# Field 5 of a recommendation model looked up instead of gathered, with the small tables as the stationary side

## What is computed

```python
wide = dense @ Wd_wide
for si, wi in zip(S, w):
    wide = wide + wi[si]
wide = wide + wc0[S[3] * VOCABS[4] + S[4]]
wide = wide + wc1[S[5] * VOCABS[6] + S[6]]
deep_in = jnp.concatenate([dense @ Wd_deep] + [Ei[si] for Ei, si in zip(E, S)], axis=1)
h = jax.nn.relu(deep_in @ W1)      # 576 -> 512
h = jax.nn.relu(h @ W2)            # 512 -> 256
deep = h @ W3                      # 256 -> 1
return bias + deep + wide
```

## Time and profile before

| what | us |
|---|---|
| median of 3 runs | 231.23 |
| profiled execution, span from first to last instruction | 134.6 |
| difference, outside the span | 96.6 |
| TensorE matmul busy | 108.5 |
| TensorE weight load busy | 88.8 |
| GpSimd busy | 94.8 |
| VectorE busy | 57.8 |
| ScalarE busy | 41.5 |
| mean granted TensorE clock (1 is full speed) | 0.918 |

### The profile page before, as it was taken

The page is one execution under the profiler, slowest core; times in us unless marked ns, Lnnn a source line. Parts: engine busy times, 40 slices in busy tenths (PEclk is TensorE's granted clock), DMA queues, the critical chain, the costliest instruction groups (busy, mean ns, idle before and its releaser), DMA issues.

```text
span 134.6 us, 2035 instructions
## 1 busy us (share of the span) xinstructions
PE 108.5 (81%) x792; PEld 88.8 (66%) x792; DVE 57.8 (43%) x136; ACT 41.5 (31%) x82; POOL 94.8 (70%) x105
## 2 busy tenths in 40 slices
PE   6978793999999999999999999999999998100000
PEld 2956782677888879888888878888878788100000
DVE  4796389218797646365622254322252234000000
ACT  3894653367631113111313313313311123000000
POOL 3688777777878778778777777777877877877400
PEclk9999999599999999999999999999999999755555
DMA  3699485233422223322334322200000000000000
GB/s 97 167 277 178 78 107 103 20 22 28 36 24 26 29 23 32 28 25 25 32 21 33 28 25 27 32 0 1 5 0 0 1 0 0 1 0 0 1 2 0
DMA packets 5993, 5.17 MB, mean 38 GB/s; under 512 B 2955, under 2 KB 4267, under 8 KB 5984
## 3 DMA queue, kind: packets, MB, share of 16 engines
q0 software_dynamic: 3072, 2.15, 20.1%
q1 hardware_dynamic: 2912, 2.90, 7.7%
HBM read 4.87 MB, written 0.17 MB: 37 GB/s over the span
## 4 chain that ended last, share of the span: by engine, by line
POOL 68%; issue 22%; DMA 3%; POOLq 1%; DVE 1%; DVEq 0%
POOL x L315 47%; POOL cross L322 21%; DMA cross<-in_wc_dram,idx_cross 2%; DMA idx_raw<-in_index_dram 1%; POOLq L99 1%; DVE idx_wrap L448 0%; DVE idx_sum L450 0%; DVE idx_look L454 0%; DVE result L623 0%; DVE idx_gather L454 0%; DVEq L622 0%
## 5 line engine op out<-in xcount | busy, mean ns | idle before, releaser
L315 POOL DMA_INDIRECT x<-in_rows_dram,idx_gather x64 | 63.4, 990 | 21.4 <-issue 19.2
L322 POOL DMA_INDIRECT cross<-in_wc_dram,idx_cross x32 | 30.3, 946 | 9.7 <-issue 9.7
L702 PE MATMUL mm_ps<-xt_hi,w_hi 128*128 128x512 f32 x64 | 28.9, 451 | 0.0
L704 PE MATMUL mm_ps<-xt_hi,w_lo 128*128 128x512 f32 x64 | 25.6, 399 | 0.0
L703 PE MATMUL mm_ps<-xt_lo,w_hi 128*128 128x512 f32 x64 | 25.3, 396 | 0.0
L502 DVE SCALAR_TENSOR_TENSOR h_lo<-mm_ps,h_hi 128x512 fp32r<-128x512 f32 x16 | 11.0, 690 | 25.9 <-ACT h_hi L348 25.9
L348 ACT ACTIVATE h_hi<-mm_ps 128x512 fp32r<-128x512 f32 x16 | 9.6, 600 | 35.0 <-PE mm_ps L704 35.0
L671 PE MATMUL look_ps<-table_parts,onehot 128*128 128x65 bf16 (+1 forms) x292 | 18.2, 216 | 2.4 <-ACT x L358 1.4
L671 PEld LDWEIGHTS look_ps<-table_parts,onehot 128*128 128x128 bf16 x292 | 15.5, 98 | 5.7 <-issue 2.9
L496 DVE TENSOR_TENSOR xt_lo<-tr_ps,xt_hi 128x512 fp32r<-128x512 f32 x16 | 11.0, 685 | 18.1 <-ACT xt_hi L342 18.1
L704 PEld LDWEIGHTS mm_ps<-xt_hi,w_lo 128*128 128x128 f32 x64 | 12.2, 190 | 2.7
(11 more groups left out here) (79 smaller groups left out, 100.7 us busy)
## 6 DMA issues: line engine op xcount, KB each, us to landing
x<-in_rows_dram,idx_gather POOLq DMA_INDIRECT x64, 3.3
w_sb<-in_w_dram SPq DMA_DIRECT2D x1, 1024.0 KB
w_sb<-in_w_dram SPq DMA_DIRECT2D x1, 512.0 KB
cross<-in_wc_dram,idx_cross POOLq DMA_INDIRECT x32, 2.4
dense_stack<-dense_dram SPq DMA_DIRECT2D x3, 156.0 KB
table<-in_small_dram SPq DMA_DIRECT2D x1, 195.0 KB, 2.5
table<-in_small_dram SPq DMA_DIRECT2D x1, 162.5 KB, 2.5
dense_dram<-dense_parts SPq DMA_DIRECT2D x1, 156.0 KB
```

The costliest lines, as they stand in the source:

```text
L315: nc.gpsimd.indirect_dma_start(out=x[:, t, g * ROW:(g + 1) * ROW], out_offset=None, in_=big[g], in_offset=bass.IndirectOffsetOnAxis(ap=idx ...
L322: nc.gpsimd.indirect_dma_start(out=cross[:, c, t:t + 1], out_offset=None, in_=wc[c], in_offset=bass.IndirectOffsetOnAxis(ap=idx_cross[:, c ...
L702: nc.tensor.matmul(dst, w_hi, a_hi, start=start, stop=False)
L704: return nc.tensor.matmul(dst, w_lo, a_hi, start=False, stop=stop)
```

## The change

- Field 5 (8 chunks of 128 rows) joins the looked-up fields; the gathers of rows are 48, in the order fields 0 and 1 of a block, then field 2 of it. The cross gathers stay.
- `look_up` is turned round. For a chunk, `table_hl` (64 columns of high parts and 64 of what is left, both fp32r) is stationary and the one-hots of 512 samples move: one fp32r matmul a chunk and block, 76 in all. The bank then holds the embeddings already turned, the high part in partitions 0 to 63 and the low one in 64 to 127, and ScalarE copies both (`looked`) into `xt_hi` and `xt_lo`. `x`, the summing by VectorE and the turns of these fields are gone; turns are two a block.
- The fields' weights are looked up apart (`look_up_wide`): 128 one-hots are stationary, the upper bf16 half of each fp32r element being read by a step of two, and the weights move as three bf16 columns. 76 such matmuls a block, 304 in all, add into three columns of `deep_ps` for each tile. VectorE adds these at the end with four small instructions more.
- One-hots are for 512 samples in fp32r, 19 chunks a block, and there is one tile of them: the next block's first one waits for `look_up_wide`.
- Only block 0's indices are spread by TensorE. Those of the others go turned to memory (`idx_dram`) and come back by three broadcast DMAs of 640 KB on SyncE's queue, ahead of W2 and of the dense parts.
- W1 comes in four loads, two of them (and the first table) from ScalarE's queue. The fields are paired anew, (0, 1), (2, 5), (3, 4), (6, 7); layer 1 goes pair by pair over four banks (`l1_ps`), and the dense matmuls come between pairs. Lookups and turns share two banks (`io_ps`), whose order of use is `IO_ORDER`; layer 2 has one bank.

```diff
-GATHERED = [0, 1, 2, 5]
-LOOKED_UP = [3, 4, 6, 7]
...
+GATHERED = [0, 1, 2]
+LOOKED_UP = [3, 4, 6, 7, 5]
...
+PAIRS = [(0, 1), (2, 5), (3, 4), (6, 7)]
+KB = len(PAIRS)
+HOME = [next((g, p.index(f)) for g, p in enumerate(PAIRS) if f in p) for f in LOOKED_UP]
+W1_ORDER = [2, 3, 0, 1]
...
+IO_ORDER = [("spread", 0, i) for i in range(NL)] + [("look", 0, i) for i in range(4)]
+IO_ORDER += [("turn", 0, 0), ("look", 0, 4)]
+for _b in range(BLOCKS):
+    if _b > 0:
+        IO_ORDER += [("look", _b, i) for i in (2, 3, 4)] + [("turn", _b, 0)]
+    if _b + 1 < BLOCKS:
+        IO_ORDER += [("look", _b + 1, 0), ("turn", _b, 1), ("look", _b + 1, 1)]
+IO_ORDER += [("turn", BLOCKS - 1, 1)]
...
+            sp.wait_ge(row_index_ready, 1)
+            sp.dma_start(idx_dram.rearrange("f (t p) -> (f t) p", p=P), row_idx[:]).then_inc(row_index_stored, 16)
+            sp.dma_start(wdense[:, H1:H1 + 1], wd_wide).then_inc(wide_weight_loaded, 16)
+            for g in (0, 1):
+                sp.dma_start(w1_sb[:, g, :], w1[D + g * P:D + (g + 1) * P, :]).then_inc(w1_loaded[g], 16)
+            sp.wait_ge(row_index_stored, 16)
+            for b in range(1, BLOCKS):
+                s = slice(b * BLOCK, (b + 1) * BLOCK)
+                sp.dma_start(idx_bc[:, :, s], idx_dram[:, s].unsqueeze(0).to_broadcast([P, NL, BLOCK]))\
+                  .then_inc(index_spread[b], 16)
...
-                for pair in range(NG // 2):
-                    for t in range(b * BT, (b + 1) * BT):
-                        for g in (2 * pair, 2 * pair + 1):
-                            nc.gpsimd.indirect_dma_start(
-                                out=x[:, t, g * ROW:(g + 1) * ROW], out_offset=None, in_=big[g],
-                                in_offset=bass.IndirectOffsetOnAxis(ap=idx_gather[:, g, t:t + 1], axis=0),
-                            ).then_inc(rows_gathered[b][pair], 16)
+                for t in range(b * BT, (b + 1) * BT):
+                    for g in (0, 1):
+                        nc.gpsimd.indirect_dma_start(
+                            out=x_pair[:, t, g * ROW:(g + 1) * ROW], out_offset=None, in_=big[g],
+                            in_offset=bass.IndirectOffsetOnAxis(ap=idx_gather[:, g, t:t + 1], axis=0),
+                        ).then_inc(rows_gathered[b][0], 16)
+                for t in range(b * BT, (b + 1) * BT):
+                    nc.gpsimd.indirect_dma_start(
+                        out=x_two[:, t, :], out_offset=None, in_=big[2],
+                        in_offset=bass.IndirectOffsetOnAxis(ap=idx_gather[:, 2, t:t + 1], axis=0),
+                    ).then_inc(rows_gathered[b][1], 16)
...
+            def looked(b, i):
+                g, half = HOME[i]
+                bank, to = io_bank(("look", b, i)), slice(half * D, (half + 1) * D)
+                act.wait_ge(io_full, IO_AT["look", b, i] + 1)
+                nc.scalar.copy(xt_hi[b % 2][to, g, :], bank[0:D, :]).then_inc(io_act, 1)
+                nc.scalar.copy(xt_lo[b % 2][to, g, :], bank[D:2 * D, :]).then_inc(io_act, 1)
...
+            act.dma_start(table[:, 0:CA], small[:, 0:CA]).then_inc(table_loaded[0], 16)
+            for g in (2, 3):
+                act.dma_start(w1_sb[:, g, :], w1[D + g * P:D + (g + 1) * P, :]).then_inc(w1_loaded[g], 16)
+            table_high_part(0)
+            for i in range(2):
+                copy_spread(i)
+            weight_high(2)
+            act.wait_ge(row_index_turned, 1)
+            nc.scalar.copy(row_idx[:], l2_ps[0:IDX_ROWS, 0:P]).then_inc(row_index_ready, 1)
+            for i in range(2, NL):
+                copy_spread(i)
+            table_high_part(1)
+            looked(0, 0)
+            looked(0, 1)
+            table_high_part(2)
+            weight_high(3)
+            act.wait_ge(wdense_done, 1)
+            nc.scalar.copy(wdense[:, 0:H1], l2_ps[0:NROWS, :]).then_inc(wdense_copied, 1)
+            looked(0, 2)
+            looked(0, 3)
...
+            turned_hi(0, 0)
             act.wait_ge(wdense_rest, 1)
             nc.scalar.copy(wdense_parts[:, 1, :], wdense[:]).then_inc(wdense_rounded, 1)
-            turned_hi(0, 0)
-            weight_high(2)
-            turned_hi(0, 1)
-            weight_high(3)
-            copy_spread(1, 0)
-            turned_hi(0, 2)
-            copy_spread(1, 1)
-            copy_spread(1, 2)
+            looked(0, 4)
             act.wait_ge(w2_loaded, 16)
             nc.scalar.copy(w2_hi[:], w2_sb[:]).then_inc(w2_high, 1)
-            turned_hi(0, 3)
-            copy_spread(1, 3)
-            copy_spread(1, 4)
+            looked(1, 0)
+            turned_hi(0, 1)
+            looked(1, 1)
...
+                relu2(b, 0)
+                if b + 1 < BLOCKS:
+                    looked(b + 1, 2)
+                    looked(b + 1, 3)
+                relu2(b, 1)
+                if b + 1 < BLOCKS:
+                    looked(b + 1, 4)
+                    turned_hi(b + 1, 0)
+                    if b + 2 < BLOCKS:
+                        looked(b + 2, 0)
+                    turned_hi(b + 1, 1)
+                    if b + 2 < BLOCKS:
+                        looked(b + 2, 1)
...
+            def build_onehot(b, i, chunks=None):
+                every = range(CHUNKS[i]) if chunks is None else chunks
+                if every[0] == 0:
+                    if b == 0:
+                        dve.wait_ge(io_act, act_count(IO_AT["spread", 0, i]))
+                    elif i == 0:
+                        dve.wait_ge(index_spread[b], 16)
+                        dve.wait_ge(looked_wide, b)
+                for c in every:
+                    nc.vector.tensor_scalar(
+                        onehot[:, CHUNK0[i] + c, :], idx_bc[:, i, b * BLOCK:(b + 1) * BLOCK], row_id[:, c:c + 1],
+                        None, ALU.is_equal).then_inc(onehot_ready, 1)
...
+            table_low_part(0)
+            build_onehot(0, 0)
+            build_onehot(0, 1)
+            w1_low_part(0)
+            build_onehot(0, 2)
+            table_low_part(1)
+            build_onehot(0, 3)
+            w1_low_part(1)
+            build_onehot(0, 4, range(0, 4))
+            table_low_part(2)
+            build_onehot(0, 4, range(4, CHUNKS[4]))
...
+            build_onehot(1, 0)
+            build_onehot(1, 1)
+            w1_low_part(3)
             turned_lo(0, 1)
...
+                if b == 0:
+                    build_onehot(1, 2)
+                    build_onehot(1, 3)
+                if b + 1 < BLOCKS:
+                    build_onehot(b + 1, 4)
+                    weigh_first(b)
+                    turned_lo(b + 1, 0)
+                    weigh_second(b)
...
+                if b + 2 < BLOCKS:
+                    build_onehot(b + 2, 0)
+                    build_onehot(b + 2, 1)
+                if b + 1 < BLOCKS:
+                    turned_lo(b + 1, 1)
+                if b + 2 < BLOCKS:
+                    build_onehot(b + 2, 2)
+                    build_onehot(b + 2, 3)
...
+            def io_free(use):
+                k = IO_AT[use]
+                if k >= IO_BANKS:
+                    pe.wait_ge(io_act, act_count(k - IO_BANKS))
+                    if dve_count(k - IO_BANKS):
+                        pe.wait_ge(io_dve, dve_count(k - IO_BANKS))
...
-            def look_up(pair, n):
...
-                        last = nc.tensor.matmul(look_ps[n % LOOK_BANKS][:, at:at + part.shape[-1]],
-                                                onehot[:, CHUNK0[i] + c, t * P:(t + 1) * P], part,
-                                                start=q == 0, stop=q == len(passes) - 1)
...
+            def look_up(b, i):
+                use = ("look", b, i)
+                io_free(use)
+                if b == 0 and i in (0, 2, 4):
+                    pe.wait_ge(table_low, 1 + i // 2)
+                for c in range(CHUNK0[i], CHUNK0[i] + CHUNKS[i]):
+                    pe.wait_ge(onehot_ready, b * NCH + c + 1)
+                    last = nc.tensor.matmul(io_bank(use)[:], table_hl[:, c, :], onehot[:, c, :],
+                                            start=c == CHUNK0[i], stop=c == CHUNK0[i] + CHUNKS[i] - 1)
+                last.then_inc(io_full, 1)
+            def look_up_wide(b):
+                if b == 0:
+                    pe.wait_ge(look_w_ready, 1)
                 for s in range(BT):
-                    last = nc.tensor.transpose(tr_ps[n % 2][:, s * P:(s + 1) * P],
-                                               x[:, b * BT + s, 2 * g * ROW + 1:2 * g * ROW + 1 + 2 * D], ident[:])
-                last.then_inc(turned, 1)
-            def wait_bank(n):
-                if n >= 2:
-                    pe.wait_ge(layer_high, n - 1)
-                    b, m = (n - 2) // TURNS, (n - 2) % TURNS
-                    if m < M1:
-                        pe.wait_ge(layer1_low, b * M1 + m + 1)
+                    for c in range(NCH):
+                        last = nc.tensor.matmul(deep_ps[:, 2:2 + SPLIT, b * BT + s],
```

(70 more changed lines are left out.)

607 lines of the change are left out of this document (209 added, 398 removed).

## The result

The kernel after takes 201.82 us (median of 4 runs, 201.46 to 203.0) where the one before takes 230.93 in the same session (229.16 to 231.69): a ratio of 0.877, 95% interval 0.872 to 0.882. The forecast was 224.0 with a range of 219.5 to 231. The sign was right; the gain is 29.1 us, four times what was forecast, and lies outside the range.

What follows compares the result with a forecast made beforehand. GpSimd's 96 gathers were taken as the bound, TensorE's work as the next limit, 13 us apart. Start 38.5, three blocks of 26.0 and the ending gave 120.8, span 127.3; plus 96.6 outside the span, 224.0 us, range 219.5 to 231.

Steps and rivals of the forecast that it cites:

- The 96.6 us: Time taken to lie outside the profiled span, added unchanged to the forecast span of 127.3 us, about 0.5 either way.
- 7.3 for the whole change: Whole kernel: the result ready at 120.8 us against 128.14, so 7.3 us less.
- The pace of a late gather: GpSimd's list: a late gather is busy for 946 ns with 0.3 us before it, 1.25 in all.
- up to 1.44: Rival: VectorE's memory work slows GpSimd to 1.44 us a gather or more, which holds the end; 224 to 230, chance 0.03.
- the 20.0 us that were to come off their end: GpSimd's chain: field 5 takes 16 gathers away, 20.0 us less, last cross value at about 107.9.
- the cheap end of the bounds: The 304 added narrow matmuls on TensorE: 0.025 to 0.101 us each, 7.6 to 30.8 us; 0.030 taken, 9.1 us.
- The rival of slow strided loads: Narrow matmuls: a step of two loses the fast load, 0.101 us each, 21.6 us more, 245.6; chance 0.15.
- half-speed ones: Rival, narrow matmuls: half of each read thrown away, pitch twice 25 ns, 6.1 us more, 230.1; chance 0.07.
- The start: From the beginning to layer 2's first half: TensorE waits for dense rows until 30, ends at 38.5, range 36 to 42.5.
- A block without a fall of the clock: TensorE's steady part: 20.06 us without lookups becomes 26.0 us a block, packed.
- The rival of the clock: Narrow stretch counts as idling, clock falls: three to four falls at 1.6 us, 228.8 to 230.4; chance 0.12.
- the 27 that the forecast named as a sign of being wrong: Profile after: a block longer than 27 us would show the forecast wrong.

Runs made afterwards that it cites:

- h1: The kernel before, unchanged, profiled on the chip of the first group: 227.2 us, span 225.4.
- h3: The kernel before with all 96 gathers left out, their tiles filled with zeros, while before took 227.3 us: 119.7 us, ratio 0.527.
- g2: The kernel before without the 16 gathers of field 5, while before took 229.3 us: 206.5 us, ratio 0.903.
- g3: The kernel after with 16 gathers more, into a tile nobody reads, while before took 229.3 us: 224.7 us, ratio 0.981.
- e1: The kernel after without its 32 cross gathers, cross values set to zero: 129.7 us, ratio to before 0.938, span 128.4.
- e0: The kernel before, unchanged, profiled once more: 137.7 us, span 135.4 in an execution of 137.3.
- e2: The kernel after with all 80 gathers left out, rows and cross values set to zero: 125.7 and 129.4 us.

## Why the prediction was wrong, step by step

**The 96.6 us.** This is the step that failed. The forecast read the difference of the median (231.2) and the span (134.6) as start and end of the execution, carried it over unchanged and gave it 0.5 us either way. It is time inside the span, of another condition than the profile's: h1 has a span of 225.4 in 227.2 us, and around the span there are 1.8 us. And it is not constant: it comes with the gathers (h3: 119.7) and shrinks when there are fewer (1.43 us each, g2 and g3). Removing 16 of them gave 22.8 us, whatever held the end, where the forecast had 7.3 for the whole change. So the sign was right by luck: "faster" was forecast because GpSimd let TensorE hold the end, and came mostly because fewer gathers starve TensorE for a shorter time. The clue stood in the table of times before: no row of the profile accounts for 42% of the time, and a span can't be judged by a time 1.7 times as long.

**GpSimd.** The pace of a late gather was right, 1.25 (0.95 busy and 0.30 before it), and there are 16 fewer. But the rows of e1 take 1.49 each (4.57 to 74.55, 48 of them) where e0's take 1.31: 21 of them are busy for 1.04 to 3.14 us, most of these beside one-hots. That VectorE can slow the gathers, which the forecast held open up to 1.44, is so, and still leaves GpSimd ahead of TensorE in e1. In the bad condition the gathers are hardly on the chain that ends last (6%) and still cost more than the 20.0 us that were to come off their end.

**The end of the span.** The forecast kept the 6.4 us between the issue of the output and the end of the span. In e0 and in the profile before, GpSimd's last gather starts at 126.35 and 125.56, and the span ends 9.0 us later in both; where the gathers end early (e1, h1, after) the span ends 1.8 us after the output's issue. So in the good condition 4.6 us more would be gained.

**TensorE's terms.** e1 is the run to judge them by (columns: start us, us, engine, line, operation, count, idle before):

```profile
24.57 1.12 PE L609 MATMUL io_ps<-ident,x_pair 128*128 128x128 f32 x4 [6.34 <-DMA x_pair<-in_rows_dram,idx_gather]
25.34 3.76 PE L586 MATMUL io_ps<-onehot,table_hl 128*128 128x512 f32 x8
...
28.90 2.15 PE L596 MATMUL deep_ps<-look_w_parts,onehot 128*128 128x3 bf16 x76
30.91 0.48 PE L613 MATMUL l_ps<-xt_hi,w_hi 128*128 128x512 f32 x1
...
42.79 1.40 PE L586 MATMUL io_ps<-onehot,table_hl 128*128 128x512 f32 x5
```

```profile
54.56 2.08 PE L596 MATMUL deep_ps<-look_w_parts,onehot 128*128 128x3 bf16 x76
...
80.27 2.08 PE L596 MATMUL deep_ps<-look_w_parts,onehot 128*128 128x3 bf16 x76
82.20 1.03 PE L670 MATMUL deep_ps<-ones,h_w 128*128 128x1 f32 x8
...
107.52 2.08 PE L596 MATMUL deep_ps<-look_w_parts,onehot 128*128 128x3 bf16 x76
```

```profile
126.34 0.17 DVE L558 TENSOR_TENSOR result<-wide_deep,cross 128x16 f32<-128x16 f32 x1
```

The narrow matmuls go at 0.025 to 0.026 us (1.93 and 2.01 for 76), at the cheap end of the bounds; 0.030 was taken. The rival of slow strided loads (0.101) and that of half-speed ones (0.050) are refuted. The Trainium skill, TensorE: Matmul & The Clock Gate, section Weight-path perf modes, said so, as the forecast cites it: a step of two keeps the fast load, and the trace agrees. One-hots take 0.48, not 0.45, and TensorE has no wait for one in e1.

The start was mis-sized: layer 2's first half ends at 42.8, forecast 38.5 with a range to 42.5. The wait is not the dense rows but the turn before them, 6.3 us for the gathers of block 0, which landed at 24.6 beside loads that keep the DMA engines busy (share 0.91 at 16 to 28 us in after's stretches above). The walk of the start had no term for those gathers; with this wait the dense rows are there in time. After it the clock was at its lower level until 28.9, and the transposes and eight lookups took 4.33 us (24.57 to 28.90) where 0.44 + 8 x 0.228 = 2.26 would be full speed: 2.1 lost, 0.8 was put down for it. The row of that stretch in e1:

```profile
24.60:28.90 4.30, 4.30 (x12) 3.20 (x13) 1.36 (x2) 1.10 (x2) 3.16 (x4) 0.50 0.71 88
```

Without gathers (e2) the first half ended at 38.3, and TensorE then waited 1.8 us for the dense rows, as the walk has it.

A block without a fall of the clock takes 25.7 us (narrow matmuls at 54.56 and 80.27), forecast 26.0. The rival of the clock came true in part: after the narrow stretches of blocks 2 and 3 the clock was granted near its lower level (1.2 GHz) for 3.4 us, after that of block 1 it was not.

```profile
84.00:87.40 3.40, 3.40 (x12) 2.72 (x11) 1.17 (x4) 1.74 (x3) 0.00 (x0) 0.52 0.00 0
87.40:92.00 4.60, 4.60 (x22) 3.76 (x21) 2.41 (x6) 1.64 (x3) 0.00 (x0) 0.99 0.00 0
...
112.40:115.80 3.40, 3.40 (x12) 2.65 (x11) 0.68 (x1) 0.27 (x1) 0.00 (x0) 0.64 0.00 0
```

Twelve matmuls in 3.4 us, where 22 take 4.6 after it. The block with such a fall in it takes 27.25 (80.27 to 107.52), 1.5 more, and over the 27 that the forecast named as a sign of being wrong.

Summed: the result in e1 is ready at 126.5, forecast 120.8; the start has 4.3 more, the two falls 3.1 more at 1.5 each, and three shorter blocks give 0.9 back, 6.5 in all, which is 0.8 more than the 5.7 us to be explained; that rest stays in rounding and small terms. With the shorter end the span is 128.4, and the forecast's own 127.3 was nearly met by two errors that cancel, which is luck. Two slips in the forecast's arithmetic did no harm: VectorE's parts add up to 13.7 us a block, not 15, and its bounds to 229.5 at the top, not 228. For the good condition the reading of TensorE would have served: 137.4 to about 130.

**What stays open.** Why one condition or the other holds for a whole group of runs; which unit withholds the instructions; why a hole begins some gathers late; and why the rest of the change gives 4.7 us under starvation while it costs 8.7 without gathers.

## What to carry to other kernels

Compare the profiled execution's own time with the times that are to be changed before using one row of it. Here only 1.8 us lie around the span in every run of either condition; with a span 97 us below the times the profile was of another condition, and no sum made from it held. Where an engine idles for "issue", look at what GpSimd does in that stretch; there, in these runs, long instructions got more done than many short ones, fewer gathers beat faster work, and a wait in GpSimd's list after every few gathers was worth more than both. Name such a remainder as a rival of its own, with what it would be if it scaled with each engine's work.
